# A fused recurrent and windowed-attention layer on one core: VectorE writes both scaled copies of the turned x ahead of the mask on G, and ScalarE copies the turned B ahead of its table load

## The reference

```
xdt   = x * dt                                   # x: 4 heads of 64, dt: one number per token and head
Acs   = cumsum(dt * A)                           # within a chunk
Lmat  = exp(segsum(dt * A))                      # lower triangular decay between two tokens
Y_diag = einsum(C, B, Lmat, xdt)                 # (C B^T, masked and decayed) @ xdt
decay_states = exp(Acs[last] - Acs)
states = einsum(B, decay_states, xdt)            # B^T @ (xdt * decay)
Y_off  = einsum(C, states_prev, exp(Acs))
y = Y_diag + Y_off
```

## Time and profile before

| what | value |
|---|---|
| median of three executions | 4362.87 us |
| profiled execution, own time | 4366.42 us |
| its span, first to last instruction | 4364.5 us |
| mean granted TensorE clock | 0.896 of full speed |
| a block (one sequence), from one mask on G to the next | 262.5 to 267.6 us |

### The profile page before, as it was taken

How to read it: one execution, slowest core, us unless ns; L and a number is a source line. 1 busy time by engine, 2 the same in 40 slices (tenths; PEclk the granted TensorE clock), 3 DMA queues, 4 the chain that set the end, 5 groups by cost and what they waited for, 6 DMA issues and landing times. The chain is left out here.

```text
span 4364.5 us, 57448 instructions
## 1 busy us (share of the span) xinstructions
PE 3328.3 (76%) x17248; PEld 1943.8 (45%) x17248; DVE 2494.5 (57%) x4239; ACT 2565.4 (59%) x5843; POOL 1724.6 (40%) x1428
## 2 busy tenths in 40 slices
PE   4677778777777777778777787777777777777777
PEld 2344444444444454444444444444444444444443
DVE  5655655656566564665546556565555656565433
ACT  4465556565656655556555665656656565565554
POOL 2353442535334353343534425354243533435332
PEclk9799899998989899898898989889899898989998
DMA  2000000000000000000000000000000000000000
GB/s 79 3 1 1 5 1 6 1 1 6 1 6 1 1 6 1 6 1 6 1 1 6 1 6 1 1 6 1 6 1 1 6 1 6 1 1 3 1 3 3
DMA packets 18387, 20.57 MB, mean 5 GB/s; under 512 B 768, under 2 KB 17152, under 8 KB 17792
## 3 DMA queue, kind: packets, MB, share of 16 engines
q1 hardware_dynamic: 18048, 16.44, 1.1%
HBM read 12.24 MB, written 4.19 MB: 4 GB/s over the span
## 5 line engine op out<-in xcount | busy, mean ns | idle before, releaser
L1446 POOL TENSOR_TENSOR hc<-hst,Cs 128x512 f32<-128x512 f32 x512 | 654.9, 1279 | 1212.4 <-DVE hst L1216 1134.7
L1216 DVE TENSOR_TENSOR_SCAN hst<-dA,bank 128x512 f32<-128x512 f32 x512 | 624.9, 1221 | 330.8 <-ACT dA L906 154.2
L560 PE MATMUL bank<-W,xs 128*128 128x512 f32 x960 | 524.9, 692 | 41.6 <-DVE tmp L1357 39.2
L912 ACT COPY Cs<-bank 128x512 f32<-128x512 f32 x512 | 298.4, 583 | 295.6 <-PE bank L543 266.8
L543 PE MATMUL bank<-parts,sel 96*128 96x512 bf16 x1024 | 360.7, 426 | 135.6 <-ACT Cs L912 60.6
L1505 POOL TENSOR_TENSOR oT<-tmp 128x512 f32<-128x512 f32 x256 | 324.5, 1268 | 331.8 <-DVE tmp L1357 183.9
L1208 DVE TENSOR_TENSOR bank<-u,bank 128x512 f32<-128x512 f32 x512 | 351.4, 686 | 181.1 <-PE bank L543 180.1
L1520 POOL TENSOR_TENSOR Pm<-Pm,rinv 128x512 f32<-128x512 f32 x256 | 271.1, 1059 | 436.2 <-DVE rinv L1370 415.5
L1042 ACT ACTIVATE Pm<-bank,mx 128x128 f32<-128x128 f32 x1024 | 363.5, 372 | 109.0 <-DVE mx L1377 109.0
L906 ACT ACTIVATE dA<-delta,neg_a 128x512 f32<-128x512 f32 x512 | 371.0, 725 | 48.2 <-DVE hst L1216 47.3
L528 PE MATMUL bank<-C,hc 128*128 128x128 f32 x2048 | 358.0, 305 | 36.2 <-POOL hc L1446 36.2
(11 more groups left out here) (223 smaller groups left out, 6122.5 us busy)
## 6 DMA issues: line engine op xcount, KB each, us to landing
W<-wpack SPq DMA_DIRECT2D x1, 4498.0 KB, 13.5
x_tok<-x SPq DMA_DIRECT2D x16, 256.0 KB, 2.9
out<-xa SPq DMA_DIRECT2D x16, 256.0 KB, 2.2
rot<-tables SPq DMA_DIRECT2D x2, 512.0 KB, 16.2
wc_f<-taps SPq DMA_DIRECT2D x1, 1024.0 KB, 19.2
C<-cpack SPq DMA_DIRECT2D x1, 721.0 KB, 14.8
Pm<-mask SPq DMA_DIRECT2D x1, 320.0 KB, 15.1
tmp<-rowpack SPq DMA_DIRECT2D x1, 256.0 KB, 17.1
```

Of the source, the lines that this page charges most:

```text
L560: mm(b[:, :], weights, rhs, start=True, stop=True).then_inc(full(ring, job), 1)
L912: nc.scalar.copy(Cs[:, k % 2, :], b[:, :]).then_inc(sem("a_Cs"), 1)
L1216: v.tensor_tensor_scan(o, a, b, 0.0, ALU.mult, ALU.add).then_inc(sem("a_h"), 1)
L1446: g_.tensor_tensor(hc[:, k % 2, :], hst[:, k % 2, :], Cs[:, k % 2, :], ALU.mult)\
```

## The change

Five things are edited.

1. `dtd` = dt times decay, a 128x16 product, is new on DVE in the head of stage A, behind `dlast`. It waits for ACT's `decay`.
2. DVE writes `xdd` itself, from the turned x in PSUM by `dtd`, beside each `xdt` by dt. That makes four instructions in place of two.
3. These four stand ahead of the mask on G and of the four products with `big2`; the mask moves from slot 6 to slot 7.
4. POOL's `xdd` instruction is gone.
5. ACT copies the turned B right behind the gate's SiLU, ahead of its table load; the two copies of `shifted` move from slot 6 to slot 8.

PSUM banks of the turned x are now released by `m_xdd` in place of `m_xdt`. The core of the diff:

```
-          + [("G", "m_M", 4), ("bt", "m_bt", 1), ("xt0", "m_xdt", 1), ("xt1", "m_xdt", 2)]
+          + [("G", "m_M", 4), ("bt", "m_bt", 1), ("xt0", "m_xdd", 1), ("xt1", "m_xdd", 2)]
...
 # ScalarE
-                tables()
                 yield 6
-                shifted(xs0, xn2, "t_xs", "m_xn", i, 1)
                 act.wait_ge(*filled("B", "bt", i))
                 b = bank("B", "bt")
                 nc.scalar.copy(btok[:, :, :], ...).then_inc(sem("m_bt"), 1)
+                tables()
+                yield 8
+                shifted(xs0, xn2, "t_xs", "m_xn", i, 1)
 # VectorE, head of stage A
                 v.tensor_tensor(dlast[:, :], b[:, 0:16], acs[:, :], ALU.subtract).then_inc(sem("m_dlast"), 1)
+                dve.wait_ge(*step("m_decay", i))
+                v.tensor_tensor(dtd[:, :], dt[:, :], decay[:, :], ALU.mult).then_inc(sem("m_dtd"), 1)
 # VectorE, stage B
-                yield 6
+                yield 7
+                for g in range(2):
+                    dve.wait_ge(*filled("B", f"xt{g}", i))
+                    b = bank("B", f"xt{g}")
+                    for name, dst, by in (("m_xdt", xdt, dt), ("m_xdd", xdd, dtd)):
+                        each_head = by[:, :].rearrange("p (q h) -> p q h", q=NT)[:, :, 2 * g:2 * g + 2]
+                        v.tensor_tensor(dst[:, :, 2 * g:2 * g + 2, :], ..., ALU.mult).then_inc(sem(name), 1)
                 dve.wait_ge(*filled("B", "G", i))
                 ...
                 v.tensor_tensor(G, G, each(c("tri"), NT), ALU.mult).then_inc(sem("m_G"), 1)
-                yield 7
                 dve.wait_ge(*step("m_G", i))
                 for q in range(NT):
                     ...
-                for g in range(2):
-                    dve.wait_ge(*filled("B", f"xt{g}", i))
-                    ...  # xdt alone
 # GpSimd
-                yield 7
-                pool.wait_ge(*step("m_xdt", i))
-                pool.wait_ge(*step("m_decay", i))
-                ...
-                g_.tensor_tensor(xdd..., xdt..., over(decay[:, :], PM), ALU.mult).then_inc(sem("m_xdd"), 1)
```

More of the change, by code:

```diff
@@ L146 @@
            a_dA=2 * NS, a_Cs=2 * NS, a_bx=2 * NS, a_h=2 * NS, a_hc=2 * NS, a_yacc=2 * NS,
-           m_xs=4, m_sz=2, m_ea=3, m_ld=4, m_L=4, m_M=4, m_Ce=3, m_xdt=2, m_sttmp=2, m_st=3, m_y2=2, m_y3=2,
+           m_xs=4, m_sz=2, m_ea=3, m_ld=4, m_L=4, m_M=4, m_Ce=3, m_xdt=2, m_xdd=2, m_sttmp=2, m_st=3, m_y2=2, m_y3=2,
            m_ysq=2, t_xs=2, f_xs=2 * NL, f_y=2 * NL, t_v=7 * NL, t_k=4 * NL, t_r=4 * NL, t_rln=4 * NL, t_clip=4 * NL, t_oT=4 * NL,
@@ L288, in build @@
         decay = sb("decay", [16])
+        dtd = sb("dtd", [16])
         etot = sb("etot", [16])
@@ L1291, in stage_b @@
                     last.then_inc(sem("m_ld"), 1)
-                yield 6
+                yield 7
[4 more added lines that the diff above has]
+                        each_head = by[:, :].rearrange("p (q h) -> p q h", q=NT)[:, :, 2 * g:2 * g + 2]
+                        v.tensor_tensor(dst[:, :, 2 * g:2 * g + 2, :],
+                                        b[:, :].rearrange("p (q h d) -> p q h d", q=NT, h=2),
+                                        each_head.unsqueeze(3).to_broadcast([P, NT, 2, PM]), ALU.mult).then_inc(sem(name), 1)
                 dve.wait_ge(*filled("B", "G", i))
```

## The result

The changed kernel takes 4419.79 us (median of 4 runs, 4417.68 to 4429.75) against 4358.74 (4 runs): ratio 1.0137, 95% interval 1.0122 to 1.0153. It is 61 us slower, 57 against the 4362.87 from which the forecast was counted. The forecast was 4371.5 with a range of 4348 to 4388, so the prediction was wrong: the sign of its sum was right, its size was not.

The account below looks back on a forecast made before the run. It took a chain of waits through four engines as the bound, with PE's clock deciding y's length. 4.5 + 6.0 - 1.9 = +8.6 us gave a profiled 4375.0 and a median of 4371.5, range 4348 to 4388.

Parts of the forecast that it names:

- the state copy: DVE's state copies, behind the products and scan step: start at 1568.15 instead of 1568.30, so 0.15 us earlier.
- holds or is too low: PE's clock at y: at 0.50 in 12 or more of 15 blocks, the forecast holds or is too low.
- the five state instructions: DVE's state work ahead of y: 2.25 us instead of 2.74, ending at 1570.40, so y starts at 1570.65.
- the cover of `dtd`: DVE, head of stage A: `dtd` and its wait fit DVE's idle time, costing nothing; uncovered up to 10 us; chance 0.05.
- The sum at slot 9's end: DVE's second instruction on y: 4.5 us later over 9 blocks, 6.0 over 6, last block 1.9 earlier; sum +8.6.
- the 6 blocks: Blocks whose clock was back at 1.00 around y's start: set at +1.0 us each, between -0.62 and +1.50.
- the row chosen for before: Time from y's start to DVE's second instruction on it, in the block shown of the kernel before: 4.01 us.
- a shift of y is passed on whole: Behind y: gate, norm, projection and first attention projections wait in one chain, so y's shift reaches the time in full.
- low "throughout and beyond y": Rival: PE low through y in 15 blocks and the projection behind, 0.5 to 1.0 us more each, 4382 to 4390; chance 0.27.

Follow-up runs that it names:

- `pool_late`: Changed kernel with POOL's scan product of slot 8 held back until DVE's first state product has read its input: 4393.43 us, ratio 1.0084 to before.
- `act_warm`: Kernel before with only ACT's edit of the change, plus 22 idle matmuls on PE ahead of the states: 4364.08 us, ratio 1.0 to before.
- `xt_last`: Changed kernel with mask on G and products with `big2` first, the four products of x last on DVE: 4322.73 us, ratio 0.9907 to before.
- `vec_only`: Changed kernel with ACT's lines from before: 4418.09 us, ratio 1.0135 to before.
- `mask6`: Changed kernel with the mask on G back in slot 6: 4396.49 us, ratio 1.0074 to before.
- `warm`: Changed kernel with idle matmuls on PE, 22 ahead of the states and 14 ahead of y: 4352.23 us, ratio 0.9983 to before.
- `mask6_warm`: `mask6` with 20 and 11 idle matmuls in PE's two gaps: 4334.39 us, ratio 0.9946 to before.
- `after_down`: Changed kernel with idle matmuls in each attention layer, 9 ahead of the last turn of P, 6 ahead of the first FFN matmul: 4430.39 us, ratio 1.0162.
- `best`: `mask6` with POOL's product held back as in `pool_late` and idle matmuls in slots 7 to 9: 4364.69 us, ratio 1.0027 to before.

## Why the prediction was wrong

*What held.* The states start 3.76 us earlier (8.59 against 12.35; 3.8 forecast), with PE idle 2.43 us ahead of them instead of 5.60 (2.4). `xdd` on DVE stands 0.60 us behind its neighbour. dA starts earlier, and the state copy gains only 0.1 us (0.15). PE is newly idle 3.6 us ahead of y (2.8 to 4.8), released by DVE's last state instruction. y ran at 0.50 in 15 of 15 blocks, the sign named for "holds or is too low", and took 5.5 us to DVE's second instruction (5.46). POOL lost 31 us (30).

*First failed step: the five state instructions.* They were to take "at least 2.1, at most the old 2.74; I take 2.25", and they take 3.07 (2130.76 to 2133.83). The term was sized with 0.42 us for each, from a block where POOL was busy with `xdd` or had its product fall into DVE's wait for the first state, as in this row of before, in the block of the earlier trace rows:

```profile
1567.14 1.27 POOL L1446 TENSOR_TENSOR hc<-hst,Cs 128x512 f32<-128x512 f32 x1 [0.17 <-POOL xdd L1474]
```

DVE's copy began at 1568.30, when this was all but done. With POOL free of `xdd`, its scan product starts the moment the scan step ends, and DVE's product with two inputs in SBUF falls on it: 1.27 instead of 0.43. y therefore starts at 16.81 and not at 15.93. `pool_late` shows it by taking the overlap away: y at 15.98 and 26 us less, of which 13 would be 0.85 x 15 and 6 are seen at slot 9's end. The Trainium skill ("SBUF — State Buffer", the entry on the shared port pair in its table of terms) says that DVE and GpSimd hold that pair for a full instruction and the loser blocks wholly. The trace agrees nearly: the product takes 0.43 + 0.85 us, all of it as duration, none as idle time, of the 0.99 us for which POOL's product runs beside it. In each of the 15 blocks it ends 0.28 us behind POOL's, where a full wait would leave 0.43.

The same effect took the cover of `dtd`. It takes 0.78 us in the median where 0.17 was forecast, and DVE's next instruction at the head of stage A comes right behind it. Its start is still 1.27 to 1.28 us behind that of `dlast` in 12 of the 15 heads behind the first (1.28 in the earlier trace rows), and 1.37 to 1.38 in three, where `dtd` took 0.99 us. So it cost next to nothing, but its cover is used up.

```profile
1736.83 2.16 POOL L1507 TENSOR_TENSOR oT<-oT,rqk 128x512 f32<-128x512 f32 x2
...
1737.79 0.17 DVE L1282 TENSOR_TENSOR dlast<-bank,acs 128x16 f32<-128x16 f32 x1 [2.36 <-ACT etot L951]
1738.25 0.77 DVE L1284 TENSOR_TENSOR dtd<-dt,decay 128x16 f32<-128x16 f32 x1 [0.28 <-ACT decay L953]
1739.07 0.69 DVE L1380 TENSOR_REDUCE mx<-bank 128x4 f32<-128x512 f32 x1
```

*The sum at slot 9's end.* The forecast added 0.50 us in 9 blocks and 1.0 in 6, 10.5 us. Measured were 15 x 1.95 = 29. The late start of y makes 13 of the difference. Another 3 come from the 6 blocks that were set at +1.0, between -0.62 and +1.50: all of them ran at the low level, the +1.50 end. And 2 come from the row chosen for before: the block shown takes 4.01 us in y, the nine blocks of its kind 3.80 in the mean.

*Second failed step, and the larger: "a shift of y is passed on whole".* 29 us at slot 9's end became 54.6 in the blocks. The step was wrong in both directions. 2 us more at slot 9 became 3.8 at the block's end in after; 2 us less became nothing in `act_warm`; `xt_last`, 1 us less, gained 3.0 a block over its 15 blocks. What the traces show in its place is that the later part of a block has a length of its own, which moves with how long the level is at 0.50 there: 47.8 us in after against 44.0 before, by the estimate above 1.9 us a block or 28 in all, where 25 are to be explained. The nearest rival, low "throughout and beyond y", had the right kind of cause, but it looked for it right behind y, and its price of 0.5 to 1.0 us a block was too small. (It also counts 6 matmuls in the two sums and the projection; the trace has 8 rows, which are 4.)

*What is shown and what is not.* Shown: the loss lies in the products on VectorE (`vec_only`); with two gaps ahead of y and a short burst between them y ran at 0.50 in all 15 blocks, and with one long gap and a short one at 1.00 in all 15 (`mask6` against `xt_last`); busy PE in those gaps gives the loss back (`warm`, `mask6_warm`); the collision with POOL costs 26 us (`pool_late`); these parts overlap and don't add up. Read from the traces, but not shown by an edit: that the low level behind slot 9 makes the rest. Not shown: what decides how much of a block behind slot 9 runs at 0.50, and so why the period falls on steps. My one trial, at the last turn of P and in the FFN, moved the low stretches (`after_down`) and so couldn't settle it.

## What to carry to other kernels

A big group of matmuls wants the work just ahead of it in one piece: moving the first part of it forward splits one gap into two and can cost more than the whole gap did, so put the new products where the later group's inputs become ready, as `xt_last` does. When an engine is relieved, look at what it will start instead and whose instruction that lands on; a longer duration, not a wait, is the sign. And a gain in the middle of a loop counts only when the loop's period shows it; where it doesn't, compare the granted clock over the whole period and not only at the place of the edit.

## What the runs showed of the hardware

The period of the overlapped block, with the clock moving between its two levels all along, gathers near four values, 262.8, 266.2, 269.7 and 273.0 us, in most of these kernels. The four are equally far apart, by 3.4 us. After stays within 269.2 to 270.0 for ten blocks, `act_warm` within 266.0 to 266.5; before itself wanders between 262.5 and 267.6. In kernels that stay on one value the low stretches stand at the same places of every block: in `best`, for one, the last of them runs from about 229.5 to 243 us. Yet 2 us less at slot 9's end moved nothing in `act_warm`, and 0.75 us more work in each block made `best` 10 us faster. A plain sum over the chain was good here to about one such step, 3.4 us x 15 = 51 us.

A DVE product of 128x16 elements with both inputs in SBUF took 0.17 us in the first head, where POOL was idle, and 0.78 us in the median of all 16: 0.61 us for work of next to nothing. In the row above it ends 0.03 us behind POOL's product. A product of 128x256 went from 0.43 to 1.27 us in the same way.
